# A small read of the adapter table on all sixteen DMA engines, ahead of batch 0's input

## The reference, cut to what matters

```python
w = weight[adapter_ids]                      # (8, 512, 512) of (16, 512, 512)
y = jnp.einsum('bij,bkj->bik', x, w)
q = y[:, 107:-1, :].mean(axis=1)
routing = softmax(q @ router_W.T + router_b)
base = y @ W.T + b
t = jnp.einsum('bsd,erd->bser', y, A)
lora = jnp.einsum('bser,eor,be->bso', t, B, routing) * 2.0
return x + base + lora
```

## Time and profile before

| | us |
|---|---|
| time, median of 3 runs | 71.77 |
| the profiled execution's own time | 72.28 |
| its span (first to last instruction of the program) | 70.6 |
| PE busy within the span | 65.2 (92%) |
| DVE busy | 42.0 (59%) |
| ACT busy | 30.4 (43%) |
| bytes moved by the DMA engines | 15.30 MB |

### The profile page before, as it was taken

How to read it: one execution, slowest core, us unless ns; L and a number is a source line. 1 busy time by engine, 2 the same in 40 slices (tenths; PEclk the granted TensorE clock), 3 DMA queues, 4 the chain that set the end, 5 groups by cost and what they waited for, 6 DMA issues and landing times.

```text
span 70.6 us, 1064 instructions
## 1 busy us (share of the span) xinstructions
PE 65.2 (92%) x374; PEld 52.2 (74%) x374; DVE 42.0 (59%) x98; ACT 30.4 (43%) x62; POOL 1.2 (2%) x10
## 2 busy tenths in 40 slices
PE   2996987999999999999999999999999999999940
PEld 1331423755699998998998988889999988889920
DVE  1000020748989999949999999994293245138230
ACT  0800032857698996658763693300330444000000
POOL 5100000000000000000000000000000000000000
PEclk9999999999999999999999999999999999999999
DMA  0459899999999999999734204224633000004922
GB/s 0 134 194 393 285 395 388 408 406 412 418 409 409 409 409 406 409 409 411 307 153 102 47 0 104 54 44 110 154 149 149 0 0 0 9 0 134 312 74 74
DMA packets 7590, 15.30 MB, mean 217 GB/s; under 512 B 800, under 2 KB 4000, under 8 KB 7584
## 3 DMA queue, kind: packets, MB, share of 16 engines
q1 hardware_dynamic: 6720, 14.64, 55.6%
q10 hardware_dynamic: 864, 0.59, 3.2%
HBM read 12.08 MB, written 2.10 MB: 201 GB/s over the span
## 4 chain that ended last, share of the span: by engine, by line
PE 80%; DMA 9%; SPq 5%; issue 1%; DVE 0%; DVEq 0%
PE ps_o L594 30%; DMA wc_raw<-in_wcT_dram 9%; PE ps_t L594 8%; PE ps_o L622 8%; PE ps_y L555 5%; PE ps_y L577 4%; PE ps_y L579 4%; PE ps_y L578 4%; SPq L199 3%; PE ps_o L555 3%; PE ps_yT L577 3%; PE ps_yT L578 3%; PE ps_yT L579 3%; PE ps_yT L588 3%; PE ps_y L594 2%; SPq L204 1%
## 5 line engine op out<-in xcount | busy, mean ns | idle before, releaser
L594 PE MATMUL ps_o<-yT_hi,az_hi 128*128 128x256 f32 (+1 forms) x52 | 15.7, 301 | 0.0
L594 PE MATMUL ps_o<-yT_lo,az_hi 128*128 128x256 f32 (+1 forms) x52 | 15.4, 297 | 0.0
L594 PE MATMUL ps_o<-yT_hi,az_lo 128*128 128x256 f32 (+1 forms) x52 | 15.4, 296 | 0.0
L404 DVE TENSOR_TENSOR wc_lo<-wc_raw,wc_hi 128x1024 fp32r<-128x1024 f32 x10 | 11.9, 1215 | 0.1
L594 PEld LDWEIGHTS ps_o<-yT_hi,az_hi 128*128 128x128 f32 x52 | 9.8, 188 | 0.4
L594 PEld LDWEIGHTS ps_o<-yT_hi,az_lo 128*128 128x128 f32 x52 | 9.8, 188 | 0.5
L594 PEld LDWEIGHTS ps_o<-yT_lo,az_hi 128*128 128x128 f32 x52 | 9.8, 188 | 0.3
L309 ACT CAST wc_hi<-wc_raw 128x1024 fp32r<-128x1024 f32 x10 | 10.0, 1050 | 0.0
L476 DVE SCALAR_TENSOR_TENSOR wc_raw<-ps_o,rest_raw,xT_raw 128x256 f32<-128x256 f32 (+1 forms) x12 | 6.2, 542 | 6.0 <-PE ps_o L622 6.0
L555 PE MATMUL ps_y<-wc_raw,xT_raw 128*128 128x512 f32 x16 | 7.4, 597 | 0.5 <-DMA wc_raw<-in_wcT_dram 0.5
L642 PE MATMUL ps_l<-warm 128*128 128x512 bf16 x11 | 4.8, 625 | 1.3 <-DVE warm L481 1.3
(11 more groups left out here) (84 smaller groups left out, 114.6 us busy)
## 6 DMA issues: line engine op xcount, KB each, us to landing
wc_raw<-in_wcT_dram SPq DMA_DIRECT2D x16, 512.0 KB, 12.3
rest_raw<-in_rest_dram SPq DMA_DIRECT2D x2, 512.0 KB, 9.7
xT_raw<-in_xT_dram SPq DMA_DIRECT2D x2, 512.0 KB, 14.3
out_dram<-wc_raw SPq DMA_DIRECT2D x2, 512.0 KB, 3.1
xT_raw<-in_xT_dram SPq DMA_DIRECT2D x3, 256.0 KB, 7.1
yT_raw<-y_turn SPq DMA_DIRECT2D x12, 64.0 KB, 2.1
out_dram<-wc_raw SPq DMA_DIRECT2D x3, 256.0 KB, 2.3
rest_raw<-in_rest_dram SPq DMA_DIRECT2D x1, 278.0 KB, 8.1
```

Of the source, the lines that this page charges most:

```text
L404: tt(flat(wc_lo[b % 2][:, part_h, :]), flat(wc_raw[:, b, part_h, :]), flat(wc_hi[b % 2][:, part_h, :]).bitcast(F32), ALU.subtract).then_in ...
L594: last = mm(bank, stat[:, n, c, :], yT[mov][:, c].rearrange("p b s -> p (b s)"), start=(start and c == 0 and k == 0), stop=(stop and c == ...
```

## The change

A tile `seen` of 16 partitions x 4 x 4 numbers is added, and one DMA that fills it, issued by ACT directly ahead of x of batch 0 and on the same queue. It reads, from adapters 0, 5, 10 and 15, the first 4 numbers (16 bytes) of the rows of partitions 0 to 15 in the first half: 64 pieces of 16 bytes, 1 KB in all. The 16 partitions are its outermost dimension. Nothing computes with `seen`. ACT waits for its arrival (`table_seen`) at the end of its program, ahead of the last half store.

```diff
+    QUEUES, SEEN_EVERY = 16, 5
...
+        seen = sb("seen", [QUEUES, -(-NADAPT // SEEN_EVERY), 4])
...
+        table_seen = sem("table_seen")
...
             act.wait_ge(ident_ready, 1)
+
+            act.dma_start(seen[:], wcT[0::SEEN_EVERY, 0, 0:QUEUES, 0, 0:4].rearrange("a p o -> p a o"))\
+                .then_inc(table_seen, 16)
             act.dma_start(flat(xT_raw[:, 0]), xT0[0]).then_inc(x_arrived(0), 16)
             act.wait_ge(warm_ready, 1)
...
             hi_tsT(LAST)
+            act.wait_ge(table_seen, 16)
             store_last_half(act, 1)
```

## The result

The kernel became slower: 72.55 us, the median of 6 runs (72.28 to 73.95), against 71.75 us for the kernel before (6 runs, 71.25 to 73.6). The ratio is 1.014, with a 95% interval of 1.010 to 1.018, so about 1.0 us (0.7 to 1.3). In part of all executions, with and without the change, the time is some 1.5 us longer; the ratios here leave those out.

What follows compares the result with a forecast made beforehand. PE was taken as the bound, its start set by the first adapter loads. Gain 0.2 less cost 0.05 us made the landing 0.15 us earlier, taking the median from 71.77 to 71.6 us; range 70.8 to 72.4.

Steps and rivals of the forecast that it cites:

- What bounds the kernel: Whole kernel: PE busy 65.2 of 70.6 us; first loads decide when it runs without a break, from 11.05 us.
- the hole of 0.77 us ahead of batch 1: PE from 10.28 to 11.05 us: waiting for the first half of batch 1's adapter, room for PE to follow an earlier landing.
- the 1.3 us between x and the adapter: Start of batch 0: delayed x still lands 1.3 us or more ahead of the adapter, so its wait stays covered.
- the sign that I had named: Trace after: PE's matmuls of batch 1 at about 10.9 instead of 11.05 us; over 0.5 us either way refutes the forecast.
- The share of the engines: DMA engines from 4.3 us: x's bytes moving beyond that delay the adapter at 409 GB/s; taken as 0.05 us lost.
- The gain: First adapter's packets at 4.3 to 5.5 us: reading the table beforehand removes slow first packets; 0.2 us, between 0 and 0.49.
- Rival A: Start-up loads: nothing gained or lost, as four later adapters stream without a dip; 71.8 us, chance 0.25.
- The deep dip at 7.0 to 8.2 us: Change from batch 0's adapter to x of batch 1: 0.50 us, assigned to x's untouched tensor, gain counted at zero.
- The small read: Queue ahead of x of batch 0: x lands at 4.7 to 5.2 us, upper bound 6.7.
- The end: ACT's last half store: the new wait on table_seen passes at once, cost zero.
- C: Start-up queue: four slow starts hold x up to 2.0 us, adding 0.64 us to the path; 72.4 us, chance 0.20.
- B: Start-up loads: all dips go, landing at 10.9 comes 1.0 us earlier; 70.8 us, chance 0.13.

Runs made afterwards that it cites:

- e1: The kernel before, unchanged, run against itself for a second trace: ratio 0.9965, 71.64 us.
- e7: The changed kernel without ACT's wait for the identity matrix, so the small read goes out earlier and x at 1.25 us: ratio 1.007.
- e12: The changed kernel with x issued ahead of the small read and 64 bytes of padding behind the tile seen: ratio 1.0003.
- e5: The kernel before without ACT's wait for the identity matrix, no small read, x issued at 0.82 us: ratio 1.002.
- e13: The kernel before, no small read or new tile; ACT waits for POOL's last mask, x issued at 1.97 us: ratio 1.011.
- e14: The kernel before, no small read; x waits for one more POOL memset (256 columns of a last tile), issued at 2.21 us: ratio 1.017.
- e17: The kernel before, no small read; x waits for a longer POOL memset (600 columns of a last tile), issued at 2.50 us: ratio 1.000.
- e3: The changed kernel with ACT's two issues swapped, x ahead of the small read: ratio 1.005.
- e10: The changed kernel with 64 bytes of padding behind the tile seen, moving later tiles by 128 bytes a partition: ratio 1.014.
- e4: The changed kernel with ACT's wait for the small read moved from the end to behind its first work on x of batch 1: ratio 1.011.
- e9: The kernel before with only an unused tile of 64 bytes a partition added, no DMA or wait: ratio 1.0048.
- e15: e10 with ACT waiting for POOL's tile of ones instead of the identity matrix, x issued at 1.66 us: ratio 1.003.

## Why the prediction was wrong

**What bounds the kernel.** Right: the loads before 11 us, and from there PE without a break. Wrong in one link: I read the hole of 0.77 us ahead of batch 1 as slack, and took it, and the 1.3 us between x and the adapter, as cover. The hole comes and goes (0.03 us in e1, 0.50 in e7, 0.78 in e12, 1.20 in e5). I had the sign of this in hand, a profiled execution 0.5 us above the median, and subtracted the 0.5 us at the end instead of asking where they lay. For the same reason the sign that I had named, PE's first matmuls of batch 1, was of no use: they begin at 11.07 us after the change and at 11.05 before, in a kernel that is 1.0 us slower.

**The tile.** The step is missing. The diff adds a tile ahead of most others; I priced the DMA, the wait and the issue, and not the 64 bytes. It measures 0.33 us, a third of the result.

**The share of the engines.** This is the term that failed most. I took 0.05 us for a shift of 0.4 us, from the bytes of x that would move past the adapter's first packets, at 409 GB/s. In the traces the shift is as forecast (x issued at 2.00), but the adapter's packets now come at 3.9, with the shorter read of the ids, and the later x costs 0.65 us (1.0 less 0.33, with the 0.06 of the end in it), in e13 0.8. It is no count of bytes: x of 256 KB is 0.64 us at most; a shift of 0.4 costs about that (0.8 in e13), one of 0.64 (e14) 1.2 us, and one of 0.93 (e17) nothing. The Trainium skill (DMA: Bandwidth & Descriptors, "Issuing engines are not separate DMA queues") says that DMAs of different issuers run on the same 16 engines and interleave; the traces agree, with q10 and q1 on the engines together at 3.8 to 4.3 us in e13. The price that I made from it, bytes over full rate, was too low in the window and too high behind it.

**The gain.** Taken as 0.2 us, none found: e2, which reads x instead of the table, costs as much as the change; e3 and e12, where the table is read in good time for the first adapter and x is on time, are at 1.000 and 1.003 less the tile. At the same late moment the kernels with a read (1.006 to 1.009, and e10) and without (1.011) overlap in their intervals, so a gain of 0.2 us there is not excluded. Rival A's argument, that four later adapters show no slow start, held. The deep dip at 7.0 to 8.2 us (237 GB/s over the whole) is not in every execution: e1 has 329 there. It is back in e5 (275) and e7 (232), which have the first adapter issued at 3.15 and 3.26, as late as the first trace (3.25), and in e4 (259); so it is not a first touch of x's tensor, and what makes it is open.

**The small read.** Right that it is cheap, and cheaper than expected: x lands 2.6 us after its issue at 2.00, at 4.6, where 4.7 to 5.2 was expected and 6.7 was the upper bound. So the read holds x up by its issue and by nothing more.

**The end.** Zero was forecast, 0.06 us were seen on ACT's last store.

**The sum.** Forecast were 0.2 gained and 0.05 lost; measured are nothing gained, 0.33 lost by the tile, 0.06 by the end and about 0.6 by the moment of x.

**The rivals.** C had the sign and nearly the size (72.4) with a chance of 0.20, but that was luck, for its mechanism was not this one: it had x held up for 2.0 us by four slow starts, and put the point of decision at a shift of 0.8 us. The shift of 0.43 us was enough, and one of 0.93 us was harmless. B did not occur.

## What to carry to other kernels

A new tile is a change of every address behind it: allocate it last (e14 and e17 have a new tile behind all others, and their stretch is 54.78 us, as without one), or time the kernel with the empty tile alone, before the rest is explained. Slack of one profiled execution that lies over the median is not slack until a second execution shows it. And two transfers of two queues that start within some tenths of a microsecond of each other can cost more than their bytes; moving one of them either way by half a microsecond is a cheaper experiment than any other here.

## What the hardware showed that I had not expected

The 64-byte shift of PE's operands costs 0.33 us in 55, and one of 128 bytes gives 0.16 back. x issued at 1.56 or at 2.50 costs nothing that can be measured, and 0.8 to 1.2 us between; issued at 0.82 or 1.25 it goes with longer reads of the ids on SP (1.08 and 1.39 us for the second, against 0.91).

The first matmuls of batch 0 can run slowly. In the profiled execution of e14 PE waited 1.94 us for the adapter, and the granted clock then fell from full (2.4 GHz) to half (1.2 GHz) while PE was already at work again (columns as in the earlier trace rows, the clock is the third value from the end):

```profile
7.00:8.00 1.00, 0.50 (x1) 0.30 (x2) 0.00 (x0) 0.00 (x0) 0.00 (x0) 1.00 0.94 295
8.00:9.00 1.00, 1.00 (x3) 0.52 (x2) 0.00 (x0) 0.00 (x0) 0.00 (x0) 0.63 1.04 395
9.00:10.00 1.00, 1.00 (x2) 0.33 (x1) 0.00 (x0) 0.00 (x0) 0.00 (x0) 0.50 1.04 424
```

```profile
7.50 5.37 PE L559 MATMUL ps_y<-wc_raw,xT_raw 128*128 128x512 f32 x8 [1.94 <-DMA wc_raw<-in_wcT_dram]
```

Its eight matmuls of batch 0 take 5.37 us, against 3.67 in the earlier trace rows. The wait doesn't explain it. In e13 they take 5.10 us behind a hole of 1.28 us, and in e3 5.35 us behind one of 1.16, with the clock full in every row; holes of 1.33 us in e1, 1.67 in e9 and 1.80 in e15 are followed by the usual 3.67 us. What brings the slow start on is open.

No version beat the kernel before. The kernel before with nothing but 128 bytes of padding, which by the stretches would save 0.16 us, was not tried.
